# First cross attention: the causal mask on DVE, the shifts on POOL; all three cross attentions: both halves of the attend behind the scores

## The reference, cut to what matters

```python
Q = q @ Wq.T + bq;  K = k @ Wk.T + bk;  V = k @ Wv.T + bv      # k is the context, 77 rows
scores = einsum('bhqd,bhkd->bhqk', Q_, K_) / D_HEAD ** 0.5
scores = where(tril, scores, -1e9)                             # causal mask, query >= key
att = einsum('bhqk,bhkd->bhqd', softmax(scores), V_)
x = layer_norm(att + q);  x = ff(x) + x
```

## Time and profile before

| what | value |
|---|---|
| median of 3 runs | 2608.63 us (2605.84 to 2609.42) |
| profiled execution | 2601.15 us, span 2599.3 us, mean granted clock 0.982 |
| PE, DVE, ACT, POOL busy | 91%, 73%, 58%, 59% of the span |
| A0 | about 0 to 412 us of the span |
| A1 | about 560 to 1000 us |
| A2 | about 1000 to 1400 us |
| A3 | about 1551 to 2440 us |

### The profile page before, as it was taken

The page is one execution under the profiler, slowest core; times in us unless marked ns, Lnnn a source line. Parts: engine busy times, 40 slices in busy tenths (PEclk is TensorE's granted clock), DMA queues, the critical chain, the costliest instruction groups (busy, mean ns, idle before and its releaser), DMA issues. The chain is left out here.

```text
span 2599.3 us, 82853 instructions
## 1 busy us (share of the span) xinstructions
PE 2368.9 (91%) x26670; PEld 1807.7 (70%) x26670; DVE 1894.2 (73%) x4003; ACT 1502.3 (58%) x3407; POOL 1537.1 (59%) x2438
## 2 busy tenths in 40 slices
PE   6999998987777777999998988999999999999899
PEld 4666666966565665777776876777777777777587
DVE  4676763139999995777775667888888888888566
ACT  4777776558888884777776533444444444444343
POOL 2555555127888884555556776666666666666332
PEclk8999999989999997999999999999999999999999
DMA  4111111234445441221111213333333333333121
GB/s 121 37 38 38 38 39 46 70 115 149 153 147 156 150 150 47 44 47 47 46 46 41 67 57 95 93 96 96 92 92 92 93 92 92 92 93 92 46 58 55
DMA packets 443043, 211.78 MB, mean 81 GB/s; under 512 B 206400, under 2 KB 433856, under 8 KB 442816
## 3 DMA queue, kind: packets, MB, share of 16 engines
q1 hardware_dynamic: 442944, 210.51, 30.3%
HBM read 113.36 MB, written 29.88 MB: 55 GB/s over the span
## 5 line engine op out<-in xcount | busy, mean ns | idle before, releaser
L666 PE MATMUL bank<-sb_ident,sb_region 128*77 128x128 f32 x3072 | 414.3, 278 | 85.5 <-ACT sb_pT L754 84.5
L666 PEld LDWEIGHTS bank<-sb_ident,sb_region 128*77 128x77 f32 x3072 | 350.8, 151 | 139.8 <-issue 137.6
L754 ACT ACTIVATE sb_pT<-bank 77x1024 f32<-77x1024 f32 x384 | 391.0, 1018 | 67.6 <-PE bank L666 67.6
L858 DVE TENSOR_REDUCE sb_max<-bank 128x8 f32<-128x616 f32 x256 | 203.5, 795 | 206.8 <-PE bank L648 118.2
L1517 ACT ACTIVATE sb_l<-sb_l 128x640 f32<-128x640 f32 x128 | 94.4, 737 | 402.2 <-DVE sb_l L1565 402.2
L749 ACT ACTIVATE sb_region<-sb_region 128x616 f32<-128x616 f32 x384 | 276.7, 720 | 1.4 <-POOL sb_region L995 1.4
L1638 POOL TENSOR_TENSOR sb_pn<-sb_l,sb_r_all 128x512 f32<-128x512 f32 x128 | 134.5, 1051 | 231.8 <-DVE sb_r_all L1575 228.0
L1398 PE MATMUL bank<-sb_region,sb_wqkv 128*128 128x128 f32 x2048 | 253.4, 277 | 1.1 <-ACT sb_region L1526 0.7
L682 PE MATMUL bank<-sb_pT,sb_v 77*32 77x128 f32 x6144 | 248.6, 280 | 3.5 <-ACT sb_pT L754 3.2
L1432 PE MATMUL bank<-sb_wvo,sb_region 128*64 128x512 f32 x1024 | 247.9, 605 | 0.0
L1398 PEld LDWEIGHTS bank<-sb_region,sb_wqkv 128*128 128x128 f32 x2048 | 241.9, 194 | 3.6 <-ACT sb_region L1526 1.3
(11 more groups left out here) (183 smaller groups left out, 5652.1 us busy)
## 6 DMA issues: line engine op xcount, KB each, us to landing
sb_region<-in_side SPq DMA_DIRECT2D x64, 616.0 KB, 3.8
sb_pT<-sb_region SPq DMA_DIRECT2D x512, 64.0 KB, 2.1
sb_kF<-sb_region SPq DMA_DIRECT2D x512, 64.0 KB, 2.1
scratch_after_A<-sb_y SPq DMA_DIRECT2D x256, 64.0 KB, 1.7
sb_fx<-scratch_after_A SPq DMA_DIRECT2D x96, 128.0 KB, 2.1
sb_mask<-in_mask SPq DMA_DIRECT2D x64, 154.0 KB, 2.2
sb_x<-scratch_after_F SPq DMA_DIRECT2D x128, 64.0 KB, 1.8
sb_ctx<-in_ctxT SPq DMA_DIRECT2D x192, 38.5 KB, 1.9
```

Of the source, the lines that this page charges most:

```text
L666: mm = nc.tensor.transpose(two[0:C, h * T:(h + 1) * T], p_s[b.par][:, head * C:(head + 1) * C], ident[:])
L754: nc.scalar.activation(pT_s[k][:], two[0:C, :], ACT.Copy).then_inc(pT_kept.sem(b), 1)
L858: nc.vector.tensor_reduce(dst, by_bank_and_head(scores_half(k)), AX.X, ALU.max).then_inc(max_made.sem(b), 1)
```

## The change

In A0 the mask matmuls go from PE; DVE adds the mask while it copies the scores out of PSUM (`add_causal`), takes the maxima from SBUF (`peak_masked`), copies the values (`keep_v`) and adds the residual row (`residual`); POOL subtracts the maxima (`shift`, in two halves) and gives up `residual`; ACT gives up `keep_v` and takes A1's order, with both `keep_pT` ahead of `keep_q`; DVE's `sum_context` goes from the head of a lap to its end. In A0, A1 and A2, PE's `attend(b, 0)` at the end of a lap becomes `attend(b-1, 0)` in the next one, between `scores(b+1)` and `attend(b-1, 1)`. The events' name `s_weighted` becomes `s_lifted`.

```diff
@@ cross_tensor
-            taken = s_weighted if ph == "A1" else shifted
+            taken = s_lifted if ph in LIFTED else shifted            # LIFTED = ["A0", "A1"]
@@ scores
-                if ph == "A0":
-                    for c in range(2, NQ):
-                        nc.tensor.matmul(bank[c][:, 0:QC], identb[:], causal[:], start=True, stop=False)
                 for c in range(NQ):
                     rows = slice(32 * c, 32 * c + 32)
                     mm = nc.tensor.matmul(bank[c][:, 0:QC], qT_s[b.par][rows, :], kblk_s[b.par][rows, :],
-                                          start=(ph != "A0"), stop=(ph != "A2"))
+                                          start=True, stop=(ph != "A2"))
@@ PE step
                 if has(1):
                     scores(b + 1)
                 if has(-1):
+                    attend(b + -1, 0)
                     attend(b + -1, 1)
...
                 if has(3):
                     transpose_x(b + 3)
-                if has(2) and ph == "A0":
-                    mask_early(b + 2, b + 1 if has(1) else None)
-                if has(0):
-                    attend(b, 0)
@@ ACT step, as it reads after, for A0
+                keep_att(b + -1)
+                exps(b, 1)
+                keep_pT(b, 0)
+                keep_k(b + 2)
+                keep_pT(b, 1)
+                keep_q(b + 2, b + 3 if has(3) else None)
+                keep_xT(b + 3)
+                exps(b + 1, 0)
@@ DVE
+            def add_causal(b, k):
+                if k == 0:
+                    dve.wait_ge(s_made.sem(b), s_made.count(ph, b))
+                half_free(b, k)
+                nc.vector.tensor_tensor(by_bank(half(p_s[b.par], k)), scores_half(k), causal32.unsqueeze(1).to_broadcast([T, 2, QC]), ALU.add)\
+                    .then_inc(s_lifted.sem(b), 1)
+            def residual(b):
+                dve.wait_ge(residual_loaded.sem(b), residual_loaded.count(ph, b))
+                wait_earlier(dve, sum_made, ph, b, 2)
+                nc.vector.tensor_tensor(xb_s[b.par][:], xr_s[b.par][:], w["bo"][:], ALU.add).then_inc(xb_made.sem(b), 1)
+            def step_causal(b, has):      # each under its has(...)
+                add_causal(b + 1, 0); add_causal(b + 1, 1)
+                invert(b + -1); peak_masked(b + 1, 0); normalise(b + -1); keep_v(b + 1)
+                sums(b + -2); peak_masked(b + 1, 1); statistics(b + -2)
+                residual(b + -1); aggregate(b + -2); sum_context(b + 1)
@@ POOL step, A0
+                    shift(b, 1); rstd(b + -3); block_keys(b + 2); centre(b + -3); shift(b + 1, 0); affine(b + -3)
@@ setup
-            nc.vector.tensor_copy(causal[:], causal32).then_inc(masks_made, 1)
```

More of the change, by code:

```diff
@@ L376, in build_layers @@
         CROSS = ["A0", "A1", "A2"]
+        LIFTED = ["A0", "A1"]
         X_loaded = event("X_loaded", CROSS, transfers=1)
@@ L561, in load_weights @@
                 if (b + -2).exists:
-                    sp.wait_ge(s_weighted.sem(b + -2), s_weighted.count(ph, b + -2, 1))
+                    sp.wait_ge(s_lifted.sem(b + -2), s_lifted.count(ph, b + -2, 1))
                 sp.dma_start(side_s[b.par][:], at(a["side"], b).rearrange("b t n -> (b t) n")).then_inc(weights_loaded.sem(b), 16)
@@ L817, in step @@
             def step(b, has):
-                weighted = ph == "A1"
+                weighted, lifted = ph == "A1", ph in LIFTED
                 if has(-1):
@@ L822, in step @@
                     keep_oT(b + -2)
-                if has(0) and weighted:
+                if has(0) and lifted:
                     exps(b, 1)
@@ L828, in step @@
                     block_keys(b + 2) if weighted else keep_k(b + 2)
-                if weighted:
-                    if has(-3):
+                if lifted:
+                    if has(-3) and weighted:
                         centre(b + -3)
@@ L841, in step @@
                     keep_xT(b + 3)
-                if has(0) and not weighted:
+                if has(0) and not lifted:
                     keep_pT(b, 1)
                 if has(1):
-                    exps(b + 1, 0 if weighted else 1)
+                    exps(b + 1, 0 if lifted else 1)
             drive(act, NB, step, reach=REACH)
@@ L871, in weigh @@
                 nc.vector.tensor_tensor(by_bank(half(p_s[b.par], k)), scores_half(k), by_bank(half(side_s[b.par], k)), ALU.mult)\
-                    .then_inc(s_weighted.sem(b), 1)
+                    .then_inc(s_lifted.sem(b), 1)
[4 more added lines that the diff above has]
+                nc.vector.tensor_tensor(by_bank(half(p_s[b.par], k)), scores_half(k), causal32.unsqueeze(1).to_broadcast([T, 2, QC]), ALU.add)\
+                    .then_inc(s_lifted.sem(b), 1)
             def mask(b, k):
-                dve.wait_ge(s_weighted.sem(b), s_weighted.count(ph, b, k))
+                dve.wait_ge(s_lifted.sem(b), s_lifted.count(ph, b, k))
                 nc.vector.scalar_tensor_tensor(half(p_s[b.par], k), half(mask_s[b.par], k), MASKED, half(p_s[b.par], k),
@@ L879, in peak_masked @@
             def peak_masked(b, k):
-                dve.wait_ge(s_masked.sem(b), s_masked.count(ph, b, k))
+                done = s_masked if ph == "A1" else s_lifted
+                dve.wait_ge(done.sem(b), done.count(ph, b, k))
                 if (b + -1).exists:
@@ L890, in keep_v @@
                 src = v_bank[0:C, V_COL:V_COL + D].rearrange("p (h v) -> p h v", v=DH)
-                nc.vector.tensor_tensor(dst, src, w["bv"][0:C, :].rearrange("p (h v) -> p h v", v=DH), ALU.add).then_inc(v_kept.sem(b), 1)
+                if ph == "A0":
+                    nc.vector.tensor_copy(dst, src).then_inc(v_kept.sem(b), 1)
+                else:
+                    nc.vector.tensor_tensor(dst, src, w["bv"][0:C, :].rearrange("p (h v) -> p h v", v=DH), ALU.add).then_inc(v_kept.sem(b), 1)
+            def residual(b):
+                dve.wait_ge(residual_loaded.sem(b), residual_loaded.count(ph, b))
+                wait_earlier(dve, sum_made, ph, b, 2)
+                nc.vector.tensor_tensor(xb_s[b.par][:], xr_s[b.par][:], w["bo"][:], ALU.add).then_inc(xb_made.sem(b), 1)
             def sum_context(b):
@@ L959, in step_weighted @@
                     aggregate(b + -2)
+            def step_causal(b, has):
+                if has(1):
+                    add_causal(b + 1, 0)
+                    add_causal(b + 1, 1)
+                if has(-1):
+                    invert(b + -1)
+                if has(1):
+                    peak_masked(b + 1, 0)
+                if has(-1):
+                    normalise(b + -1)
+                if has(1):
+                    keep_v(b + 1)
+                if has(-2):
+                    sums(b + -2)
+                if has(1):
+                    peak_masked(b + 1, 1)
+                if has(-2):
+                    statistics(b + -2)
+                if has(-1):
+                    residual(b + -1)
+                if has(-2):
+                    aggregate(b + -2)
+                if has(1):
+                    sum_context(b + 1)
             def step(b, has):
-                if has(1) and ph == "A0":
-                    sum_context(b + 1)
                 if has(-3):
@@ L981, in step @@
                     key_bias(b + 2)
-            drive(dve, NB, step_weighted if ph == "A1" else step, reach=REACH)
+            drive(dve, NB, {"A0": step_causal, "A1": step_weighted, "A2": step}[ph], reach=REACH)
         def cross_gpsimd(pool, ph):
@@ L1037, in step @@
                         scale_mean(b + -3)
+                    if has(1):
+                        shift(b + 1, 0)
+                    if has(-3):
+                        affine(b + -3)
+                elif ph == "A0":
+                    if has(0):
+                        shift(b, 1)
+                    if has(-3):
+                        rstd(b + -3)
+                    if has(2):
+                        block_keys(b + 2)
+                    if has(-3):
+                        centre(b + -3)
                     if has(1):
@@ L1896, in _ @@
             pe.wait_ge(zeroed, N_ZERO)
-            pe.wait_ge(masks_made, 3)
+            pe.wait_ge(masks_made, 2)
             def before_self(pe):
                 pe.wait_ge(keys_placed, 4)
-                pe.wait_ge(masks_made, 4)
+                pe.wait_ge(masks_made, 3)
                 pe.wait_ge(weights_scaled, 3)
```

8 lines of the change are left out of this document (3 added, 5 removed).

## The result

The changed kernel takes 2773.57 us (median of 4 runs, 2769.48 to 2778.8) against 2607.24 us (4 runs, 2603.51 to 2609.42): a ratio of 1.064, 95% interval 1.062 to 1.066. It is slower by 166 us, where 111 was forecast (2718, range 2670 to 2750). The profiled execution has a span of 2771.4 us and a mean granted clock of 0.948; before it was 0.982.

What follows compares the result with a forecast made beforehand. Cycles of waits between engines, not PE's busy share, were taken to bound the laps. A0 39, A1 35 and A2 35 us sum to 109 on 2601.15, 2710 profiled; median forecast 2718 us, range 2670 to 2750.

Steps and rivals of the forecast that it cites:

- The first attend is on the ring in A1 and A2: A1, A2: attend lengthens the cycle of waits through keep_q and the scores that sets the lap; 0.58 us, 35 us each.
- A0's ring through ACT: A0: cycle of waits from the scores over transposes, both keep_pT and keep_q to the next scores; 6.78 us a lap.
- the ring through POOL: A0: cycle from keep_k over POOL's keys, centring, shifts and affine, ACT's exponentials, to next keep_k; 6.95 us a lap.
- The two rings of A0: A0: two cycles of waits, 6.78 and 6.95 us, set the lap; 6.9 taken against 6.22, costing 39 us.
- The 0.87 us of masks that PE lost: A0: four mask matmuls a lap leave PE; their 0.87 us was forecast to become idle time.
- The clock: Rival: PE's clock falls to its lower level for part of A0, time beyond 2760 us; chance 0.04.
- DVE held by POOL and the late context: Rival, A0: residual waits for POOL's shift, context lands late; lap 7.4 us, A0 costs 67, time 2746; chance 0.12.
- PE was the bound of A0: Rival, A0: saved mask time shortens the lap to about 5.6 us; with attends free, 2573 us; chance 0.05.
- The attend's move is free: Rival, A1 and A2: slack hides the attend, only A0 pays, 2648 us; one phase free, 2683; chance together 0.12.
- the floor: A0: POOL's own work, the least a lap can take; forecast at 5.59 us from busy times.

Runs made afterwards that it cites:

- attend_at_the_end: Changed kernel with the first attend put back at the end of PE's lap in all three phases, new A0 kept; 2647.45 us, ratio 1.016.
- only_the_attend_moved: Kernel before the change with only the first attend moved behind the scores; 2729.80 us, ratio 1.047.
- keys_behind_the_shift: attend_at_the_end with POOL's keys and centring behind shift(b+1, 0) in A0; 2632.61 us, ratio 1.011.
- query_ahead_of_second_copy: attend_at_the_end with ACT's keep_q ahead of the second keep_pT in A0; 2652.17 us, ratio 1.018.
- filler_in_a1: Changed kernel with three unread matmuls in PE's idle time ahead of the scores, in A1 only; 2700.94 us, ratio 1.036.
- sum_behind_the_adds: attend_at_the_end with, in A0, POOL's keys behind the shift, keep_q ahead of the second keep_pT, and DVE's sums right behind the adds; 2618.84 us, ratio 1.005.
- the second filler: Changed kernel with three unread matmuls in PE's shorter idle time ahead of A1's second transposes; 2717.84 us, ratio 1.043.

## Why the prediction was wrong

- *The first attend is on the ring in A1 and A2*: right, shown by attend_at_the_end and only_the_attend_moved. The size was too large: 0.58 us was taken, while a pair of attends takes 1.01 us, so the second costs 0.43. At full clock it is 23.4 us in A1 and 27.2 in A2, for 35 each. The same 1.01 stands in A0's ring through ACT, which comes to 6.63 us instead of 6.78; the ring through POOL was the longer one either way.
- *The two rings of A0*: right. The lap is 6.9 us as forecast, with the attend in either place, A0's own order costs 40 us for 39 forecast, POOL waits for `keep_k`, and its ring is the longer one (keys_behind_the_shift against query_ahead_of_second_copy). The 0.87 us of masks that PE lost bought nothing here: PE now idles 1.40 us ahead of the scores.
- *The clock*: this is the step that failed. The sum had no term for it. The rival gave it a chance of 0.04, looked for it in A0 alone, and argued from the 1.00 that A1 had at 79% busy. It is A1 that lost it, 65.4 us by filler_in_a1. A0 lost another 9 us, 434.0 against 425.4 with the attend back, in three laps of 9.2 us among those of 6.9 and in some at the start; with the attend back its clock is 1.00 from 100 to 450 us, against 0.97. The two together are more than the 55 us between forecast and result; the attend's smaller size takes the rest away. The trace before showed the place, 1.1 us of idle time ahead of the scores in A1, longer than in A0 or A2. The prediction took the attend out of just that gap and priced only the engine's time.
- The Trainium skill (TensorE: Matmul & The Clock Gate, "HAM oscillation — how this bites in real kernels") describes a matmul loop that waits for its DMA in every round and falls to the lower clock in every round. The trace agrees in part: A1 falls in 24 laps of 61, to a mean of 0.82, and what PE waits for there is ACT's `keep_q` and no DMA. A0, with 72% of busy time on PE, kept 0.97.
- *DVE held by POOL and the late context*: not what sets the changed kernel. There `sums` takes 0.29 us at the mean and `residual` 0.34, and no projection of keys waits for a DMA between 100 and 455 us. Both appeared once the rings were opened, and sum_behind_the_adds, without the late context and with less of the hold, has the same laps of 6.40 us.
- *PE was the bound of A0*: ruled out, since A0 is slower with less work on PE. *The attend's move is free*: ruled out in A1 and A2, where the lap grows by 0.43 and 0.44 us; in the new order of A0 it is free at full clock.

What stays open is why the clock falls in A1 and hardly in A0, which has less busy time, what exactly the second filler changed, and what holds A0 at 6.4 us once its rings are open.

## What to carry to other kernels

Before moving PE's work out of an idle time, ask what idle time is left, and give the loss of the clock a price: here one attend, moved by one place, lengthened A1's lap by 0.43 us, which cost 23 us of the phase, and the clock cost 65. A busy share of 93% did not make PE the bound of A0; follow each engine's lap back over one round, since the ring with the longest sum sets the lap and a rival ring shows only once that is opened. For a chain of small instructions on POOL, count from start to start less what it waits for others, and not by busy time: the floor was 5.8 us by the timeline and 5.6 by the busy times. And compare phases of two traces only with the medians beside them, since one execution can be the slowest and the other the fastest.

## What the runs showed of the hardware

- The same lap of A1 takes 7.2 us at the full clock and 9.5 to 10.0 us when the clock falls in it (mean 0.65 in one of 9.67 us); three matmuls that serve nothing, 0.83 us of PE's time a lap, take 65 us off a phase of 500.
- The clock fell in 24 laps of 61 with 1.63 us of idle time ahead of the scores (the median), in nine with 1.52 and in none with 1.09 or 0.81.
- Of two attends in a row, the second costs 0.43 us and one alone 0.58.
- A DVE sum of two 128x128 SBUF tiles took 1.13 us when it started 0.24 us into a POOL instruction of 1.22 us that also reads SBUF, and 0.28 us elsewhere: it ended 0.15 us behind POOL's.
